# Two whole-array bf16 products of 512 columns ahead of every unit of scores and of second products in the narrow-head attention layers

## The chip, the cores and the metric

The kernel runs on one core of a Trainium2 chip. The metric is device microseconds of one execution; lower is better. The core has TensorE (PE in the profile, its weight loads PEld), VectorE (DVE), ScalarE (ACT), GpSimd (POOL) and SyncE (SP, which issues the DMAs).

## What is computed

Twelve decoder blocks in a row on x of shape (4, 256, 256), each followed by `x = layernorm(x + block(x))`. Two of the twelve are self-attention with sixteen narrow heads, and these two are what the change touches. In block 0 (L0_attn) a head has 16 features; with `scale = 1/sqrt(16)`:

```python
scores = einsum('bhqd,bhkd->bhqk', q, k) * scale
scores = where(causal, scores, -inf)
out = einsum('bhqk,bhkv->bhqv', softmax(scores), v) @ w_proj + b_proj
```

Block 6 (L2_attn) is differential attention: 16 heads with two sets of queries and keys of 8 features each, so 32 causal score matrices per sequence, `diff = A1 - lam * A2`, a root-mean-square over the 16 features of each head, and a projection. The other ten blocks (two state-space scans, four wide attentions, four feed-forwards) stay as they are.

## The kernel before

All five engines run through the blocks in the same order and meet in semaphores. Each engine's queue is in program order. The class `SmallHeads` serves block 0 (name L0a, 4 groups of four heads, width 16) and block 6 (name L2a, 8 groups of four, width 8). A unit is one group of four heads on one sequence of 256 tokens: 16 units in L0a, 32 in L2a. Each unit has four PSUM banks, and `slot = 4 * (u % 2)` swaps the lower four and the upper four between neighbouring units.

First comes a loop of `score(u)` over all units, which finds the largest score of each row. TensorE waits until VectorE has reduced unit u - 2 (`maxed`), writes the causal mask into the four banks with four bf16 products of the identity with `causal_bf`, 256 columns each (L386), and adds eight fp32 score products (L389; the trace has two instructions for each fp32 product). Those use only 16 (L0a) or 8 (L2a) of the 128 rows of the array; four of them stand side by side, one in each strip of 32 rows. VectorE takes the maxima in two reductions (L490). After every four units `turn_max` transposes the maxima (L395), ScalarE copies them (L551), and SyncE moves them by DMA into row `width` of the queries, so that the second scores come out less their maximum.

Then comes a loop in which `score_t(u + 1)` stands ahead of `sum_up(u)`. `score_t` (L414) writes transposed scores, again on 17 or 9 rows in four strips; it waits for `exped` and for `sum_read`, VectorE's copy (L498) of the sums of unit u - 2. ScalarE exponentiates (L558), GpSimd zeroes the masked half (L584), and `sum_up` (L425) multiplies by the values, with 128 rows and four strips of 32 columns. Its sums lie in columns 384 to 511 of the first two banks of the slot. After the loop the sums are transposed (L440), divided, transposed again, projected (L454) and handed to `LayerNorm`.

Ahead of both loops stand the query and key projections (L364) and the value projections (L369), which are whole-array fp32 products. Elsewhere in the kernel, in block 11, twelve bf16 products of 512 columns with the identity (L1916) stand between small products.

Of the kernel before, what the change touches and what calls it, by code (L numbers as in the profile page):

```python
# [26 lines left out]
P = 128  # L27
# [16 lines left out]
class Chain:  # L44


    def __init__(self, sem):
        self.sem, self.n, self.base = sem, 0, None
# [51 lines left out]
def bcast(ap, axis, n):  # L100

    shape = list(ap.shape)
    return ap.unsqueeze(axis).broadcast_to(shape[:axis] + [n] + shape[axis:])
# [139 lines left out]
class SmallHeads:  # L243
# [10 lines left out]
    def __init__(self, e, l, arena, name, groups, width, scale, diff):  # L254
        self.e, self.l, self.name = e, l, name
        self.groups, self.width, self.scale, self.diff = groups, width, scale, diff
        self.per_block, self.units = 32 // width, 4 * groups
        a, big = arena, e.big
        a.reset(), big.reset()
        self.qk_w = a.take(groups, 2, CH, P)  # L260
        self.v_w = a.take(CH, D)
        self.proj_w = a.take(CH, D)
        self.probs_t = a.take(2, 4, 4 * P)
        self.compact_w = self.probs_t.rearrange("p u j t -> p (u j t)")[:, 0:8 * P].rearrange("p (k s c f) -> p k s c f", k=2, s=2, c=CH)
        self.inv = a.take(2, 32)
        if not diff:
            self.qk_b = a.take(2, 2)
            self.v_b = a.take(D)
            self.proj_b = a.take(D)
        self.q = big.take(groups, TOKENS)  # L270
        self.k = big.take(groups, TOKENS)
        q_words = self.q.rearrange("p g t -> p (g t)")
        k_words = self.k.rearrange("p g t -> p (g t)")
        self.v = big.take(TILES, 16, 32)
        self.stage = big.take(2, 2, TOKENS)
        self.out_first = big.take(TOKENS)
        self.max_cols = big.take(2, 4, TILES)
        self.max_rows = big.take(groups, P, parts=32)
        self.att = k_words[:, 0:TILES * 64 * groups].rearrange("p (t d) -> p t d", t=TILES)
        self.att_t = q_words[:, (groups - 2) * TOKENS:groups * TOKENS].rearrange("p (c t) -> p c t", c=CH)  # L280
        self.att_out = self.att
        if diff:
            self.att_out = k_words[:, 4096:6144].rearrange("p (t d) -> p t d", t=TILES)
            self.sq = k_words[:, 6144:8192].rearrange("p (n d) -> p n d", d=16)
            self.lam_in = a.take(4, width)
            self.lam_prod = a.take(2, width)
            self.lam_dot = a.take(2)
            self.lam_exp = a.take(2)
            self.lam = a.take(1)
            self.ms = a.take(TILES * 16)  # L290
            self.rms = a.take(TILES * 16)
        self.n_loads = 16 * (4 if diff else 5 + 4 * groups)
        s = e.sem
        self.w_loaded, self.prepared = s(name + "_w_loaded"), s(name + "_prepared")
        self.cleared, self.x_biased = s(name + "_cleared"), s(name + "_x_biased")
        self.v_psum, self.v_ready = s(name + "_v_psum"), s(name + "_v_ready")
        self.proj_psum, self.staged = s(name + "_proj_psum"), s(name + "_staged")
        self.moved = [s(f"{name}_moved{b}") for b in range(2)]
        self.scored, self.maxed = s(name + "_scored"), s(name + "_maxed")
        self.max_psum, self.max_read, self.rows_moved = s(name + "_max_psum"), s(name + "_max_read"), s(name + "_rows_moved")  # L300
        self.scored_t, self.exped, self.masked = s(name + "_scored_t"), s(name + "_exped"), s(name + "_masked")
        self.summed, self.sum_read = s(name + "_summed"), s(name + "_sum_read")
        self.turned, self.normed = s(name + "_turned"), s(name + "_normed")
        self.att_t_psum, self.att_t_ready = s(name + "_att_t_psum"), s(name + "_att_t_ready")
        if diff:
            self.lam_dots, self.lam_exps = s(name + "_lam_dots"), s(name + "_lam_exps")
            self.diffed, self.squared = s(name + "_diffed"), s(name + "_squared")
            self.msq, self.rooted, self.att_ready = s(name + "_msq"), s(name + "_rooted"), s(name + "_att_ready")
# [44 lines left out]
    def tensor(self, pe):  # L353
        e, nc, l = self.e, self.e.nc, self.l
        B, G, mm = e.bank, self.groups, self.e.nc.tensor.matmul
# [17 lines left out]
        def score(u):  # L373
            g, b = divmod(u, 4)
            slot = 4 * (u % 2)
            if u < 2:
                pe.wait_ge(*((self.v_ready, 4) if u else (self.staged, 8)))
            else:
                pe.wait_ge(self.maxed, u - 1)
            if b == 0 and g % self.per_block == 0:  # L380
                pe.wait_ge(self.moved[g // self.per_block], 16 * 8 * self.per_block)
            if b == 1 and g:
                pe.wait_ge(self.max_read, g)
            for j in range(4):
                blocks = B[slot + j][:, 0:3 * P].rearrange("p (a b) -> p a b", b=P)
                mm(blocks[:, 0:3:2, :], e.ident_bf[:], bcast(e.causal_bf[:, P:2 * P], 1, 2), start=True, stop=False, skip_group_check=True)  # L386
            for h in range(2):
                for j in range(4):
                    last = mm(B[slot + j][:, h * P:(2 * h + 1) * P], self.q[self.rows(j), g, b * SEQ + h * P:b * SEQ + (h + 1) * P],  # L389
                              self.k[self.rows(j), g, b * SEQ:b * SEQ + (h + 1) * P], start=False, stop=True, skip_group_check=True)  # L390
            last.then_inc(self.scored, 1)
# [5 lines left out]
        for u in range(self.units):  # L397
            score(u)
            if u % 4 == 0 and u:
                turn_max(u // 4 - 1)  # L400
        turn_max(G - 1)

        def score_t(u):
            g, b = divmod(u, 4)
            slot = 4 * (u % 2)
            if u == 0:
                pe.wait_ge(self.rows_moved, 16 * 4 * (G + 1))
            if u >= 2:
                pe.wait_ge(self.exped, 2 * (u - 2) + 2)
                pe.wait_ge(self.sum_read, u - 1)  # L410
            for kc in range(2):
                for j in range(4):
                    rows = self.rows(j, 1)
                    last = mm(B[slot + j][:, kc * SEQ:kc * SEQ + (2 - kc) * P], self.k[rows, g, b * SEQ + kc * P:b * SEQ + (kc + 1) * P],  # L414
                              self.q[rows, g, b * SEQ + kc * P:(b + 1) * SEQ], start=True, stop=True, skip_group_check=True)
            last.then_inc(self.scored_t, 1)

        def sum_up(u):
# [8 lines left out]
            last.then_inc(self.summed, 1)  # L427

        score_t(0)
        for u in range(self.units):  # L430
            if u + 1 < self.units:
                score_t(u + 1)
            sum_up(u)
# [1783 lines left out]
```

## Time and profile before

| | |
|---|---|
| time, median of 3 runs | 2746.41 us (2738.42 to 2749.94) |
| profiled execution, own time | 2746.3 us |
| its span | 2744.5 us |
| mean granted TensorE clock | 0.803 |
| TensorE matmul busy | 2074.4 us (76%) |
| VectorE busy | 1602.8 us (58%) |
| ScalarE busy | 787.7 us (29%) |
| GpSimd busy | 570.8 us (21%) |

L0a lies at about 24 to 170 us of the span and L2a at about 885 to 1175 us. Rows of groups and timelines name a line, an engine, an operation and its output and inputs, then the count. [...] Busy time of TensorE counts an instruction from its start to its modelled end, whatever part of the array it fills. Times are microseconds unless marked ns.

### The profile page before, as it was taken

To read this page: it belongs to the slowest core of one execution; us is meant where nothing else is said; L and a number is where in the kernel's file an instruction comes from. 1 tells how busy PE (TensorE), PEld (TensorE's weight loads), DVE (VectorE), ACT (ScalarE), POOL (GpSimd) and SP (SyncE) were. 2 spreads that over 40 slices of the span, in tenths; PEclk is the share of its full clock that TensorE was granted. 3 is DMA by queue.
4 is the path that set the end of the run, shared out by engine and by line. 5 is a ranking of instruction groups with operands and counts; after the bars stand their busy time and mean duration, and the time that the engine had idled before them with its cause. 6 is when DMAs were issued, how large, how long until landed. Compare 5 with 4: busy or idle time off the path is not lost.

```text
span 2744.5 us, 27737 instructions
## 1 busy us (share of the span) xinstructions
PE 2074.4 (76%) x9734; PEld 1308.8 (48%) x9734; DVE 1602.8 (58%) x2454; ACT 787.7 (29%) x1999; POOL 570.8 (21%) x325
## 2 busy tenths in 40 slices
PE   6774659746636888788888974454799999999986
PEld 3541234412213446566666743333566675555843
DVE  3259965879977441445555339999366514444214
ACT  1233311233312014355555211111255403444010
POOL 1212530005410003233333115655100000000010
PEclk9566879658867655689999986776799999999966
DMA  3000011010010210000001010000000100000000
GB/s 99 6 32 0 0 15 37 5 48 0 0 39 3 32 41 1 1 20 11 11 11 54 1 69 0 0 0 0 4 10 10 43 8 12 11 11 20 1 31 16
DMA packets 25727, 48.98 MB, mean 18 GB/s; under 512 B 6262, under 2 KB 19603, under 8 KB 24092
## 3 DMA queue, kind: packets, MB, share of 16 engines
q1 hardware_dynamic: 25644, 47.85, 5.8%
q8 instruction: 55, 0.90, 0.1%
q14 instruction: 28, 0.23, 0.0%
HBM read 42.20 MB, written 1.05 MB: 16 GB/s over the span
## 4 chain that ended last, share of the span: by engine, by line
PE 55%; DVE 34%; ACT 4%; issue 4%; SPq 1%; POOL 1%; DMA 1%; DVEq 0%; ACTq 0%; POOLq 0%
DVE big L789 7%; PE banks L1110 7%; PE banks L1079 7%; PE banks L1119 6%; PE banks L1048 6%; DVE big L1790 5%; PE banks L1102 3%; PE banks L414 3%; DVE big L1786 3%; PE banks L389 3%; PE banks L425 2%; PE banks L1344 2%; PE banks L386 2%; DVE big L784 2%; DVE big L770 1%
## 5 line engine op out<-in xcount | busy, mean ns | idle before, releaser
L1185 DVE COPY arena<-banks 128x512 f32<-128x512 f32 x196 | 135.5, 691 | 329.4 <-PE banks L1102 326.3
L218 POOL TENSOR_TENSOR ln_rstd<-ln_var_eps,neg_half 128x2 f32<-128x2 f32 x48 | 36.9, 768 | 1065.5 <-DVE ln_var_eps L206 1065.5
L1079 PE MATMUL banks<-big 128*128 128x256 f32 x784 | 235.7, 413 | 6.0 <-ACT big L1221 4.4
L1110 PE MATMUL banks<-arena,big 128*128 128x256 f32 x784 | 227.7, 414 | 6.3 <-DVE arena L1185 6.3
L1242 ACT ACTIVATE arena<-banks,arena 128x256 f32<-128x256 f32 x392 | 193.4, 500 | 61.0 <-DVE arena L1159 43.1
L789 DVE TENSOR_TENSOR_SCAN big<-big 128x2048 f32<-128x2048 f32 x32 | 203.4, 6355 | 1.1
L701 PE MATMUL banks<-big,ident 128*128 128x512 f32 x288 | 171.3, 750 | 38.1 <-POOL big L862 38.1
L862 POOL TENSOR_TENSOR big<-big 128x2048 f32<-128x2048 f32 x32 | 144.8, 4525 | 251.7 <-DVE big L789 251.7
L1048 PE MATMUL banks<-x_feat,arena 128*128 128x512 f32 x392 | 176.3, 592 | 0.0
L1119 PE MATMUL banks<-arena,big 128*128 128x256 f32 x784 | 174.3, 382 | 1.9 <-ACT big L1260 1.9
L1260 ACT ACTIVATE big<-banks 128x256 f32 (+1 forms) x196 | 75.3, 384 | 347.9 <-PE banks L1110 347.9
L1110 PEld LDWEIGHTS banks<-arena,big 128*128 128x128 f32 x784 | 140.8, 197 | 64.5 <-DVE arena L1185 42.9
L1166 DVE TENSOR_SCALAR arena<-arena 128x256 f32<-128x256 f32 x392 | 166.0, 466 | 6.9
L1153 DVE TENSOR_REDUCE arena<-banks 128x2 f32<-128x512 f32 x196 | 134.0, 684 | 61.6 <-PE banks L1079 43.5
L1119 PEld LDWEIGHTS banks<-arena,big 128*128 128x128 f32 x784 | 147.5, 190 | 27.5 <-issue 4.6
L1750 PE MATMUL banks<-ident,big 128*128 128x128 f32 x128 | 30.0, 426 | 161.8 <-POOL big L1839 161.8
L1079 PEld LDWEIGHTS banks<-big 128*128 128x128 f32 x784 | 136.1, 201 | 33.9 <-ACT big L1221 8.8
L1790 DVE SCALAR_TENSOR_TENSOR big<-big,arena 128x2048 f32<-128x2048 f32 x32 | 141.2, 4411 | 1.1
L1102 PE MATMUL banks<-ident,arena 128*128 128x128 f32 x784 | 127.4, 288 | 17.1 <-DVE arena L1166 17.1
L199 DVE TENSOR_TENSOR x_tok<-x_tok,banks 128x512 f32<-128x512 f32 x48 | 32.8, 683 | 182.6 <-PE banks L1119 100.1
L701 PEld LDWEIGHTS banks<-big,ident 128*128 128x128 f32 x288 | 66.9, 243 | 134.7 <-issue 75.7
L234 ACT ACTIVATE x_feat<-banks 128x512 f32<-128x512 f32 x48 | 27.8, 594 | 355.6 <-PE banks L226 355.6
(311 smaller groups left out, 3706.7 us busy)
## 6 DMA issues: line engine op xcount, KB each, us to landing
big<-big SPq DMA_DIRECT2D x32, 64.0 KB, 2.3
arena<-in_L0f_w SPq DMA_DIRECT2D x1, 2048.0 KB, 8.1
arena<-in_L1a_wo SPq DMA_DIRECT2D x1, 2048.0 KB
arena<-in_L1f_gv SPq DMA_DIRECT2D x1, 2048.0 KB
arena<-in_L2a_qk_w SPq DMA_DIRECT2D x1, 2048.0 KB
big<-big SPq DMA_DIRECT2D x64, 32.0 KB
arena<-in_L2x_wo SPq DMA_DIRECT2D x1, 2048.0 KB
arena<-in_L2x_q_w SPq DMA_DIRECT2D x16, 128.0 KB, 2.0
```

Source lines behind the costliest of these rows:

```text
L701: last = nc.tensor.matmul(B[4 + q][:], e.ident[:], self.out[k][:, q * BANK:(q + 1) * BANK], start=False, stop=False, skip_group_check=True)
L789: v.tensor_tensor_scan(self.state[k], self.decay[k], self.drive, 0.0, ALU.mult, ALU.add).then_inc(self.s_scanned, 1)
L862: self.e.nc.gpsimd.tensor_tensor(halves(self.out[k]), halves(self.state[k]), bcast(self.c_all[k], 1, CH), ALU.mult).then_inc(self.s_outed, 1)
L1048: last = mm(B[half][:], self.q_w[:, head_par, c, :], e.x_feat[:, c, cols], start=(c == 0), stop=(c == CH - 1))
L1079: last = mm(ps[:, h * SEQ:(h + 1) * SEQ], q[:, b * SEQ + h * P:b * SEQ + (h + 1) * P], k[:, b * SEQ:(b + 1) * SEQ], start=True, stop=not s ...
L1102: last = nc.tensor.transpose(B[4 + u % 2][:, kc * SEQ + h * P:kc * SEQ + (h + 1) * P], self.probs[:, u % 2, h, kc * P:(kc + 1) * P], e.ide ...
L1110: last = mm(slot, self.v[:, 2 * b + kc, :], self.probs_t[:, u % 2, kc, :], start=(kc == 0), stop=(kc == 1))
L1119: last = mm(e.y_bank(t), self.out[:, h, t * P:(t + 1) * P], wo[h], start=(h == 0), stop=(h == self.heads - 1 and not self.bias))
L1166: last = v.tensor_scalar(self.probs[:, u % 2, h, :], self.probs[:, u % 2, h, :], self.inv[:, u % 2, h:h + 1], None, ALU.mult)
L1185: v.tensor_copy(self.probs_t[:, u % 2].rearrange("p a b -> p (a b)"), B[4 + u % 2][:]).then_inc(self.turn_read, 1)
L1242: last = a(self.probs[:, u % 2, h, :], B[2 + u % 2][:, h * SEQ:(h + 1) * SEQ], ACT.Exp, bias=self.neg_max[:, u % 2, h:h + 1], scale=scale, ...
L1790: v.scalar_tensor_tensor(self.chosen[h], self.sums, self.final[:, h, 7:8], self.sums, ALU.is_ge, ALU.mult, accum_out=self.kept[:, h:h + 1] ...
```

## The change

Ahead of the mask products of each `score(u)`, and ahead of the products of each `score_t(u)`, behind that unit's waits in both cases, TensorE now makes two bf16 products of the identity with the causal block repeated four times, 128 rows by 128 columns by 512 columns each. They go to the first two banks of the slot, with `start=True`; the products behind them overwrite what is read later. Nothing waits for them by semaphore, and no wait is added or removed. In L0a that is 2 x 32 products, in L2a 2 x 64.

```diff
         self.inv = a.take(2, 32)
+        self.warm = bcast(e.causal_bf[:, P:2 * P], 1, 4)
         if not diff:
...
             if b == 1 and g:
                 pe.wait_ge(self.max_read, g)
+            for j in range(2):
+                mm(B[slot + j][:], e.ident_bf[:], self.warm, start=True, stop=True)
             for j in range(4):
                 blocks = B[slot + j][:, 0:3 * P].rearrange("p (a b) -> p a b", b=P)
...
             if u >= 2:
                 pe.wait_ge(self.exped, 2 * (u - 2) + 2)
                 pe.wait_ge(self.sum_read, u - 1)
+            for j in range(2):
+                mm(B[slot + j][:], e.ident_bf[:], self.warm, start=True, stop=True)
             for kc in range(2):
                 for j in range(4):
                     rows = self.rows(j, 1)
```

## Rows read from the trace of the kernel before

**Rows 1.** The page: span, and TensorE busy and its granted clock in 40 slices.
```profile
span 2744.5 us, 27737 instructions
...
PE   6774659746636888788888974454799999999986
...
PEclk9566879658867655689999986776799999999966
```

**Rows 2.** Windows of the narrow layers: stretch, length, busy by engine, clock, DMA share.
```profile
47.90:57.40 9.50, 7.76 (x104) 4.46 (x103) 8.68 (x12) 0.27 (x1) 0.00 (x0) 1.00 0.33 57
57.40:87.00 29.60, 28.61 (x222) 15.06 (x220) 19.07 (x22) 0.53 (x2) 0.00 (x0) 0.50 0.01 3
98.00:152.00 54.00, 44.35 (x580) 32.55 (x572) 6.37 (x15) 21.23 (x29) 18.40 (x30) 0.50 0.01 2
915.40:1003.00 87.60, 84.36 (x647) 44.66 (x647) 56.52 (x62) 1.87 (x7) 0.00 (x0) 0.50 0.09 14
1014.00:1126.00 112.00, 92.86 (x1204) 68.69 (x1200) 12.74 (x30) 44.16 (x59) 37.90 (x60) 0.50 0.03 11
```

**Rows 3.** Timeline of L2a's score loop: start, length, engine, line, idle before and releaser.
```profile
915.51 1.01 PE L386 MATMUL banks<-causal_bf,ident_bf 128*128 128x256 bf16 x4 [6.73 <-DMA big<-big]
...
918.05 1.03 PE L386 MATMUL banks<-causal_bf,ident_bf 128*128 128x256 bf16 x4
919.01 1.67 PE L389 MATMUL banks<-big 8*128 8x128 f32 x16
920.61 1.03 PE L386 MATMUL banks<-causal_bf,ident_bf 128*128 128x256 bf16 x4
920.74 1.82 DVE L490 TENSOR_REDUCE big<-banks 128x4 f32<-128x512 f32 x2 [0.74 <-PE banks L389]
```

**Rows 4.** Timeline of L0a's score loop at the full clock, with one `turn_max`, and its end.
```profile
47.94 0.60 PE L386 MATMUL banks<-causal_bf,ident_bf 128*128 128x256 bf16 x4
49.34 0.61 PE L386 MATMUL banks<-causal_bf,ident_bf 128*128 128x256 bf16 x4
51.35 0.61 PE L386 MATMUL banks<-causal_bf,ident_bf 128*128 128x256 bf16 x4 [0.54 <-DVE big L490]
53.08 0.61 PE L386 MATMUL banks<-causal_bf,ident_bf 128*128 128x256 bf16 x4 [0.25 <-DVE big L490]
53.62 0.94 PE L389 MATMUL banks<-big 16*128 16x128 f32 x16
54.81 0.61 PE L386 MATMUL banks<-causal_bf,ident_bf 128*128 128x256 bf16 x4 [0.25 <-DVE big L490]
57.27 0.80 PE L386 MATMUL banks<-causal_bf,ident_bf 128*128 128x256 bf16 x4 [0.45 <-ACT big L551]
...
85.24 1.67 PE L389 MATMUL banks<-big 16*128 16x128 f32 x16
```

**Rows 5.** Timeline of the second loop: its start in L0a, one round in L2a.
```profile
93.42 2.94 PE L414 MATMUL banks<-big 17*128 17x256 f32 x32 [4.18 <-DMA big<-big]
97.42 0.87 PE L425 MATMUL banks<-arena,big 128*32 128x128 f32 x12 [1.05 <-POOL arena L584]
...
1053.24 1.66 PE L414 MATMUL banks<-big 9*128 9x256 f32 x16 [0.64 <-DVE big L498]
1054.84 1.51 PE L425 MATMUL banks<-arena,big 128*32 128x128 f32 x24
1054.96 1.51 ACT L558 ACTIVATE arena<-banks 128x768 f32<-128x768 f32 x2 [2.23 <-PE banks L414]
1056.41 0.42 DVE L498 COPY big<-banks 128x256 f32<-128x256 f32 x1 [3.32 <-PE banks L425]
```

**Rows 6.** Timeline of block 11: whole-array products (L1908, L1916) beside products of one row (L1909).
```profile
2628.53 2.08 PE L1908 MATMUL banks<-arena,x_feat 128*128 128x256 f32 x4
2630.54 1.22 PE L1909 MATMUL banks<-arena,ones 1*128 1x256 f32 x2
2631.69 2.08 PE L1908 MATMUL banks<-arena,x_feat 128*128 128x256 f32 x4
...
2647.48 4.81 PE L1916 MATMUL banks<-arena,ident_bf 128*128 128x512 bf16 x12
```

**Rows 7.** Windows: block 11's alternation, and L2a's projections in two stretches.
```profile
2621.00:2646.00 25.00, 24.74 (x51) 13.00 (x50) 2.82 (x3) 3.37 (x5) 2.59 (x2) 0.50 0.00 0
885.40:890.40 5.00, 4.97 (x6) 2.18 (x7) 0.00 (x0) 2.08 (x3) 3.51 (x1) 0.50 0.13 30
890.40:908.00 17.60, 17.60 (x57) 10.48 (x56) 2.27 (x6) 4.18 (x7) 0.00 (x0) 1.00 0.27 41
```

## The prediction

> **What bounds the kernel now.** I read the page first. TensorE is the busiest engine, and its granted clock is far from full in several slices [rows 1]. Two of the low stretches are the narrow-head layers, so I read windows over them [rows 2]. L0a's score loop begins at clock 1.00 and runs at 0.50 from 57.4 us on; its second loop, and both loops of L2a, run at 0.50 throughout. In the score loops TensorE is busy nearly all the time (84.36 of 87.60 us in L2a) while VectorE has gaps: TensorE is the bound there. In the second loops TensorE is busy 92.86 of 112.00 us, so the timeline has to say what fills the rest.
>
> In a score unit at 0.50 the mask products start at 918.05, the narrow products at 919.01 and the next unit's mask at 920.61: 0.96 + 1.60 = 2.56 us, with no wait of TensorE, and VectorE idle 0.74 us before its 1.82 us [rows 3]. At clock 1.00 a unit takes 1.73 us (53.08 to 54.81), and TensorE waits 0.25 us of it for VectorE [rows 4]. The second loop is one closed chain through two engines: L414 starts at 1053.24, L425 at 1054.84, VectorE copies at 1056.41 for 0.42 us, and the next L414 would start 0.15 us later, at 1056.98. A round is 1.60 + 1.57 + 0.57 = 3.74 us [rows 5]. ScalarE's 1.51 us runs beside L425 and has 2.23 us of idle before it, so it sets nothing.
>
> **The change part by part.** Each unit gets 1024 more whole-array bf16 columns in each loop. At 0.50 their price is in the mask products, which are 1024 columns of the same operand and take 0.96 us up to the start of the narrow ones [rows 3]. That holds one switch from whole array to strips, which the added pair shares with the mask behind it. Twelve products of 512 columns, at 0.50 up to a rise near their end, take 4.81 us with their tail, 0.80 a pair at least [rows 6]. In the score loop the switch is shared, so the price lies below 0.96, and the last of the twelve ran at the higher clock, so it lies above 0.80: I take 0.85, nearer to the row with the same shape, bounds 0.80 and 0.96. In the second loop nothing whole-array stands behind the pair, so the switch comes on top where the wait for VectorE hid it before: 0.94, bounds 0.85 and 1.05. At full clock I take half, 0.43. None of it can be hidden by a wait in steady state: TensorE's queue is in order, and the pair stands behind the unit's waits and ahead of products that others wait for. A gain below nothing is possible only through the clock, which is the whole question.
>
> *Does the clock rise?* What counts isn't how busy TensorE is: it is busy over 95% of L2a's score loop at 0.50 [rows 2]. The nearest row is in block 11: four whole-array products for 2.01 us, then two on one row for 1.15 us, round after round, 24.74 of 25.00 us busy, and the clock stays at 0.50 [rows 6, 7]. There 64% of the time goes to whole-array work. With the change, a score unit of L2a has 0.85 + 0.96 = 1.81 us of whole-array work in 3.41 us, 53%, and the rest on 8 rows of each strip. That is less than the row that stays low. On the other side, uninterrupted whole-array work is at 0.50 for 5.00 us and at 1.00 after it [rows 7], and the twelve L1916 products in block 11 are uninterrupted too. L2a's first unit comes after 6.73 us of waiting for a DMA [rows 3], so it starts low and I expect it to stay low to the end of its scores. In its second loop a round becomes 4.68 us: the pair is 0.85 us of that, L425's column strips 1.57 with their tail, L414 on 9 rows 1.60, and the round trip to VectorE still 0.57 idle. I expect 0.50 there as well, and in L0a's second loop, which starts after 4.18 us of DMA wait [rows 5].
>
> L0a's score loop differs. It comes straight from whole-array projections at 1.00 and held it for five units with the mask alone [rows 2, 4]. There the pair doubles the whole-array columns of a unit while the unit hardly grows, so I expect the full clock to hold to its end. The unit's length there follows from the loop over two buffers: two units took 3.46 us (51.35 to 54.81); with 0.43 more ahead of the mask, 3.89, so 1.94 a unit. TensorE's own work would be 1.40 (47.94 to 49.34) + 0.43 = 1.83, less than that. A `turn_max` adds 2.46 - 1.73 = 0.73 [rows 4]. The loop ends at 47.94 + 15 x 1.94 + 3 x 0.73 + 0.43 + 1.48 (53.08 to the end of L389) = 81.1, against 85.24 + 1.67 = 86.9 now: 5.8 us less. What follows is the same transpose, copy and DMA.
>
> [...]
>
> *The sum.* L0a scores -5.8. L0a second loop 15 x 0.94 = +14.1; one of its 16 pairs, unit 1's, is hidden in the 1.05 us in which TensorE waits for GpSimd before the first L425 [rows 5]. L2a scores 32 x 0.85 = +27.2. L2a second loop 31 x 0.94 = +29.1. Together +64.6 us. The profiled execution took 2746.3 us (span 2744.5 and 1.8 around it), the median of the runs is 2746.41, so both give 2811. DMA waits ahead of and between the loops keep their length, since what they wait for moves with them.
>
> **The rivals.** A, the other sign: the pairs lift the clock in all four loops. It decides as soon as the clock is granted once in a loop, since at full clock the same pairs fill a larger share of a shorter unit, and it would hold from there. Scores in L2a go from 2.56 to 1.94 a unit, 32 x -0.62 = -19.8, with 7 turns at 0.1 more each; a round of the second loop from 3.74 to about 2.9 (1.60 and 1.57 lose the half of their streaming, about 0.64 each, and 0.43 comes in), 46 x -0.84 = -38.6. With L0a's -5.8: -63.5, 2683. For it: the clock did hold in L0a while whole-array work was in every unit. Against it: the loops start low, and a row with a larger whole-array share stays low.
>
> B: only L0a's second loop is lifted; it has 17 rows where L2a has 9, and is the nearest to it. Then 15 x -0.84 = -12.6 in place of +14.1: +37.9, 2784.
>
> C: L0a's score loop doesn't hold the full clock either; it falls as now. Then it costs 16 x 0.85 = +13.6 (less at its start) in place of -5.8: +84, 2830. Against it: the pair is the same kind of work that held it for five units.
>
> D: the pairs cost next to nothing, hidden in the 0.57 us round trip and VectorE's slack: 2746, no change. Against it: the order of the queue, as above. The price bounds (0.80 to 0.96 for 32 pairs, 0.85 to 1.05 for 46) move the forecast by -6 to +9 us.
>
> **How the numbers follow.** Forecast 2811 with chance 0.76; A 0.06; B 0.08; C 0.06; D and the rest 0.04. The forecast's own range is 2800 to 2822: the bounds of the prices, and the phase at which the clock changes in the later layers, for which the 11.5 us between the runs of before are the measure. Reaching to B leaves out less than 0.2: 2782 to 2823. A change of 0.5% is 14 us, about what a measurement of this kernel can tell from none. Slower by more: forecast, B, C and some of the rest, 0.91. Faster: A, 0.07. Same: 0.02.
>
> **What the profile after would show.** Right: L2a's score unit at 3.41 us with no wait of TensorE and clock 0.50 over the whole loop; the second loop's round at 4.68 us with the VectorE copy's releaser unchanged; L0a's scores at 1.00 up to about 81 us, units of 1.94. Wrong: clock 1.00 inside L2a's loops (A), or in L0a's second loop alone (B); a fall of the clock before 81 us (C); L414 starting sooner than 0.85 us behind the first added product (D). What would undo the forecast is one thing: that narrow or strip-wise products count for more towards the clock than the block 11 row lets me think.

## The result

| | before | after |
|---|---|---|
| time, median | 2743.44 us (4 runs, 2738.42 to 2749.94) | 2814.75 us (4 runs, 2810.12 to 2816.47) |
| profiled execution: time, span | 2746.3, 2744.5 us | 2810.12, 2808.3 us |
| mean granted clock, as a share of full speed | 0.803 | 0.800 |
| TensorE matmul busy | 2074.4 us | 2140.7 us |
| VectorE busy | 1602.8 us | 1602.5 us |

The ratio is 1.0256, with a 95% interval of 1.0228 to 1.0284: 2.6% slower. The forecast was 2811 us. The medians are 71.3 us apart and the profiled executions 63.8 us.

The page of the kernel after, the same rows as [rows 1]; lines in between are left out:

```profile
span 2808.3 us, 28121 instructions
...
PE   6874669746636888878888885544599999999986
...
PEclk9566879668867555578888998777699999999966
```

Windows of the kernel after over the stretches of [rows 2] (stretch, length, busy of TensorE, its weight loads, VectorE, ScalarE and GpSimd, clock, DMA share and GB/s): L0a's scores, its second loop, L2a's scores, its second loop.

```profile
47.30:79.80 32.50, 30.42 (x356) 16.86 (x353) 27.98 (x32) 0.80 (x3) 0.00 (x0) 1.00 0.10 19
98.00:152.00 54.00, 46.58 (x476) 26.95 (x480) 4.92 (x12) 16.62 (x22) 14.55 (x23) 0.50 0.01 1
923.80:1039.00 115.20, 111.88 (x711) 54.38 (x711) 56.64 (x63) 1.86 (x7) 0.00 (x0) 0.50 0.07 11
1050.00:1190.00 140.00, 120.86 (x1264) 69.94 (x1260) 12.72 (x30) 45.36 (x60) 38.26 (x61) 0.50 0.02 8
```

One loop of the four has the full clock, L0a's scores, to their end; the other three are at 0.50 over the whole stretch, as before. The timeline of L2a's scores after, the counterpart of [rows 3]. The added pair is L386 here, the mask L389 and the narrow products L392:

```profile
927.20 1.03 PE L386 MATMUL banks<-causal_bf,ident_bf 128*128 128x512 bf16 x2
928.02 1.06 PE L389 MATMUL banks<-causal_bf,ident_bf 128*128 128x256 bf16 x4
929.01 1.67 PE L392 MATMUL banks<-big 8*128 8x128 f32 x16
930.61 1.03 PE L386 MATMUL banks<-causal_bf,ident_bf 128*128 128x512 bf16 x2
930.75 1.82 DVE L495 TENSOR_REDUCE big<-banks 128x4 f32<-128x512 f32 x2 [1.59 <-PE banks L392]
```

From pair to pair it is 3.41 us (2.56 before), TensorE doesn't wait in these units (only at each of the seven transposes of the maxima, 0.4 us, as before), and VectorE's idle before a unit has grown from 0.74 to 1.59 us, by the 0.85 that the pair takes. The second loop after, beside [rows 5]. The pair is L415, the scores L419, the sums L430:

```profile
121.80 1.01 PE L415 MATMUL banks<-causal_bf,ident_bf 128*128 128x512 bf16 x2 [0.64 <-DVE big L503]
122.74 1.66 PE L419 MATMUL banks<-big 17*128 17x256 f32 x16
124.33 1.51 PE L430 MATMUL banks<-arena,big 128*32 128x128 f32 x24
125.91 0.42 DVE L503 COPY big<-banks 128x256 f32<-128x256 f32 x1 [4.26 <-PE banks L430]
126.45 0.14 PEld L415 LDWEIGHTS banks<-causal_bf,ident_bf 128*128 128x128 bf16 x2 [1.06 <-ACT arena L563]
126.48 1.01 PE L415 MATMUL banks<-causal_bf,ident_bf 128*128 128x512 bf16 x2 [0.64 <-DVE big L503]
```

A round is 4.68 us where it was 3.74. The pair stands between the wait for VectorE's copy and the scores, and takes 0.93 to 0.94 us up to them.

Stage by stage, each from its first TensorE product to the first one of the next stage:

| stage | before | after | difference | forecast |
|---|---|---|---|---|
| L0a scores | 47.94 to 93.42: 45.5 | 47.15 to 86.45: 39.3 | -6.2 | -5.8 |
| L0a second loop | 93.42 to 154.23: 60.8 | 86.45 to 161.55: 75.1 | +14.3 | +14.1 |
| L2a scores | 915.51 to 1009.70: 94.2 | 923.80 to 1045.31: 121.5 | +27.3 | +27.2 |
| L2a second loop | 1009.70 to 1130.35: 120.7 | 1045.31 to 1195.29: 150.0 | +29.3 | +29.1 |
| sum | | | +64.7 | +64.6 |

The profiled executions differ by 63.8 us, so all that is left for the rest of the kernel is -0.9. The medians differ by 7.5 us more than that. The profiled execution after is the fastest of its four and the profiled one before is above its median, and the times before spread over 11.5 us; which stages the other executions differ in was not traced.

### The profile page after: what moved, and what is told of

It is laid out like the page before. It is cut to its first block, busy times and chain, and to the rows that moved or that the text cites. A ratio compares the mean times of both kernels' runs of the same rounds, so it can differ in the third digit from the quotient of the medians.

```text
span 2808.3 us, 28121 instructions
## 1 busy us (share of the span) xinstructions
PE 2140.7 (76%) x9926; PEld 1319.4 (47%) x9926; DVE 1602.5 (57%) x2454; ACT 787.5 (28%) x1999; POOL 570.4 (20%) x325
## 4 chain that ended last, share of the span: by engine, by line
PE 56%; DVE 33%; issue 3%; ACT 3%; SPq 1%; POOL 1%; DMA 1%; DVEq 0%; ACTq 0%; POOLq 0%
DVE big L794 7%; PE banks L1115 7%; PE banks L1084 7%; PE banks L1124 6%; PE banks L1053 6%; DVE big L1795 5%; PE banks L1107 3%; PE banks L419 3%; DVE big L1791 3%; PE banks L430 2%; PE banks L392 2%; PE banks L1349 2%; PE banks L415 2%; DVE big L789 1%; DVE big L775 1%
## 5 line engine op out<-in xcount | busy, mean ns | idle before, releaser
L1265 ACT ACTIVATE big<-banks 128x256 f32 (+1 forms) x196 | 75.1, 383 | 347.9 <-PE banks L1115 347.9
L503 DVE COPY big<-banks 128x256 f32<-128x256 f32 x48 | 20.4, 424 | 213.7 <-PE banks L430 213.7
L589 POOL TENSOR_SCALAR_AFFINE_SELECT arena<-arena 128x512 f32<-128x512 f32 x96 | 60.9, 634 | 371.8 <-ACT arena L563 368.6
```

## The experiments

The forecast held, but its reason was my argument from neighbouring rows, which no row shows by itself: that whole-array work is what the clock goes by, that a pair a unit is too little to lift it, and that it might hold it. The rivals say that narrow loops stay low whatever stands between (so each product is only a price), or that only pauses, in which TensorE waits, take the clock away. All edits below are against the changed kernel unless said otherwise, and products are of the pair's kind.

**The pairs in L0a's scores alone.** The second loops' pairs are gone, and L2a's scores have none.

```diff
-            for j in range(2):
-                mm(B[slot + j][:], e.ident_bf[:], self.warm, start=True, stop=True)
+            for j in range(0 if self.diff else 2):
+                mm(B[slot + j % 2][:], e.ident_bf[:], self.warm, start=True, stop=True)
...
-            for j in range(2):
-                mm(B[slot + j][:], e.ident_bf[:], self.warm, start=True, stop=True)
```

> The pairs stand in the score loop of L0a alone; all other loops are as before. My theory: this is the one loop in which they pay, because it comes straight from the projections at the full clock and the pairs keep it there. L0a's scores end 5 to 6 us sooner (last score product at about 80 us instead of 86.9), the rest of the layer runs as before, and the time is about 6 us under the kernel before, 2737. Rival (the pairs only cost their own time, and the earlier end in the changed kernel came from something else): 16 x 0.43 to 0.85 us more, 2750 to 2757.

The window over L0a's scores:

```profile
47.50:80.00 32.50, 30.42 (x355) 16.86 (x353) 28.03 (x32) 0.80 (x3) 0.00 (x0) 1.00 0.10 19
```

The stage did as expected: full clock to the end, the last score product at 80.2 us. The time did not: 2749.33 us (10 runs, 2748.45 to 2750.57) against 2750.81 for before (19 runs on the same chip, 2736.58 to 2756.65), ratio 0.9991, 0.9974 to 1.0008. No gain is measured, where I had expected 2737. In its profile the first sums of L0a are turned at 147.4 us instead of 154.2, and L2a still begins 2.1 us later, at 887.5 instead of 885.4: the gain went between the two layers. The next run shows where most of it went.

**The kernel before once more**, nothing changed. It was run to see whether block 3, a stage between the two layers that the change doesn't touch, varies by itself.

> The kernel before, profiled once more, with nothing changed. My theory: the blocks between L0a and L2a hold stretches whose clock depends on where in time they fall, so that the same instructions take several us more or less; the third attention (L1a, block 3), 69.0 us in the profile of before and of the changed kernel and 74.6 us in four experiments, should take one of these two times here as well, with the narrow layers at 45.5 and 60.8 us (L0a) as before. Rival (the edits of the experiments made block 3 slower): 69.0 here.

2750.04 us. Windows of this profile: L0a's scores in two parts, and the end of block 3 (L1a), output products that alternate with bias products of one row. Under them, block 3's end in the first profile of before.

```profile
46.50:64.60 18.10, 14.88 (x202) 8.45 (x201) 16.42 (x20) 0.53 (x2) 0.00 (x0) 1.00 0.18 32
64.60:80.80 16.20, 15.75 (x124) 8.29 (x121) 10.94 (x12) 0.27 (x1) 0.00 (x0) 0.50 0.01 4
541.00:557.20 16.20, 15.40 (x36) 7.80 (x36) 9.39 (x28) 1.79 (x3) 3.06 (x4) 0.50 0.00 1
```

```profile
545.00:555.80 10.80, 9.95 (x33) 5.56 (x32) 9.35 (x28) 1.82 (x4) 2.87 (x4) 0.69 0.01 2
```

The loop of scores and the second loop of L0a in this profile begin with these:

```profile
46.22 0.60 PE L386 MATMUL banks<-causal_bf,ident_bf 128*128 128x256 bf16 x4
...
87.31 1.24 PE L414 MATMUL banks<-big 17*128 17x256 f32 x8 [4.17 <-DMA big<-big]
```

Two things come out. Block 3 took 74.5 us in this run, from its input's last copy into `x_feat` to its output's, and 69.1 in the first profile, with the same instructions: its end ran at 0.50 here (541.0 to 557.2 us) and partly at 1.00 there (1.00 from 541.0 to 548.0, 0.50 from 550.0 to 555.8). So the experiments' edits did not slow it, and that half of my theory holds. The other half doesn't: I expected L0a as in the first profile, and its scores held the full clock for 18.4 us from their start instead of 9.5, and took 41.1 us (46.22 to 87.31) instead of 45.5. They also began 1.7 us sooner, so their end, at 80.8 instead of 86.9, is no measure of the loop. The gain of about 6 us that I forecast for the pairs in L0a's scores is against one execution in which the clock fell early; against this one it is 41.1 - 39.3 = 1.8 us. What all six profiles with pairs there show is the clock held to the end of that loop, in 39.3 us. What that is worth in time depends on when the clock would have fallen.

**Six products ahead of each unit, in all four loops.** Three times the added work. The same edit stands in both loops:

```diff
-            for j in range(2):
-                mm(B[slot + j][:], e.ident_bf[:], self.warm, start=True, stop=True)
+            for j in range(6):
+                mm(B[slot + j % 2][:], e.ident_bf[:], self.warm, start=True, stop=True)
...
```

> Six products of 512 columns ahead of each unit in all four loops, three times what the change has. My theory: the clock goes by how much of a stretch is whole-array work, so six lift it from 0.50 inside every loop, and all four run at 1.00 after a few units. Then TensorE's part of a score unit is 1.40 + 6 x 0.213 = 2.68 us (2.56 at 0.50 without any), a round of the second loop is about 2.45 + 1.28 = 3.73 us (3.74 at 0.50 without any); with some units at 0.50 at each loop's start the time is 2750 to 2775: three times the added work, and 40 to 60 us faster than the pairs. Rival (narrow loops stay at 0.50 whatever stands between, every product is paid at 0.43 us): 64 units of 6 x 0.427 = 2.56 us in L2a and 16 in L0a's second loop, 1.3 in L0a's scores: 2743 + 220 = 2965.

2781.05 us, one run, beside 2750.81 for before. It is 6 us above my range, and 184 below the rival's 2965. Windows: both loops of L0a, then of L2a, each from where the clock is high:

```profile
50.00:93.00 43.00, 41.66 (x399) 21.91 (x401) 27.36 (x30) 0.80 (x3) 0.00 (x0) 1.00 0.06 11
112.60:166.00 53.40, 43.56 (x665) 25.80 (x663) 5.94 (x14) 21.17 (x28) 17.84 (x28) 1.00 0.01 2
945.40:1032.00 86.60, 83.46 (x803) 44.07 (x799) 54.72 (x60) 1.87 (x7) 0.00 (x0) 1.00 0.06 10
1051.20:1163.00 111.80, 92.52 (x1377) 54.51 (x1375) 12.72 (x30) 45.34 (x60) 37.58 (x59) 1.00 0.01 2
```

The expectation's 0.213 and 0.427 us a product stand on no row as such. The runs show 0.216 at 1.00 (thirty in a row in the next run's bridge take 6.64 us, the last of them 0.38) and 0.42 at 0.50 (this run's first six in L2a's scores take 2.72, the last of them 0.61).

This is the clearest run against "each product is only a price". With six, the clock rises by itself 9.0 to 12.4 us into each of the three loops that start low, and stays. Nor does the busy share decide it here. TensorE is busy 96% of L2a's score loop here at 1.00 (83.46 of 86.60 us), as it was before at 0.50 (84.36 of 87.60), and in the stretch ahead of the rise it is no busier than in the changed kernel, whose clock stays low (this run first):

```profile
936.40:945.40 9.00, 8.95 (x40) 3.96 (x44) 1.82 (x2) 0.00 (x0) 0.00 (x0) 0.50 0.30 47
```

```profile
924.00:937.00 13.00, 13.00 (x88) 6.58 (x86) 5.47 (x6) 0.00 (x0) 0.00 (x0) 0.50 0.33 51
```

Two rounds of L2a's second loop:

```profile
1102.84 1.46 PE L415 MATMUL banks<-causal_bf,ident_bf 128*128 128x512 bf16 x6 [0.64 <-DVE big L503]
1104.23 0.94 PE L419 MATMUL banks<-big 9*128 9x256 f32 x16
1105.09 0.86 PE L430 MATMUL banks<-arena,big 128*32 128x128 f32 x24
1106.59 1.46 PE L415 MATMUL banks<-causal_bf,ident_bf 128*128 128x512 bf16 x6 [0.64 <-DVE big L503]
```

A round is 3.75 us with 3072 added columns at the full clock, 4.68 with 1024 at the half, and 3.74 with none. The pair is the dose between: in the three loops that start low it pays its price and gets nothing back. The starts of the loops don't explain the time above my range: the four stages together are 26.4 us longer than in the profile of before, and the spans 34.6. The other 8.2 us lie in the rest of the kernel, 5.6 of them in block 3, which is at the longer of its two times here.

Every product added in these experiments is of one kind, whole-array, bf16 and 512 columns long. No run adds products on few rows, or fp32 ones, so that the rows count, and not the type or the length, is argued from block 11 and not shown.

**Bridges over the pauses, with the pairs and without.** The changed kernel with products in the time in which TensorE waits ahead of the low loops:

```diff
+            for j in range((30 if self.diff else 0) if u == 0 else 0):
+                mm(B[j % 4][:], e.ident_bf[:], self.warm, start=True, stop=True)
             if b == 0 and g % self.per_block == 0:
                 pe.wait_ge(self.moved[g // self.per_block], 16 * 8 * self.per_block)
...
+        pe.wait_ge(self.maxed, self.units - 1)
+        for j in range(8):
+            mm(B[j % 4][:], e.ident_bf[:], self.warm, start=True, stop=True)
         turn_max(G - 1)
...
+            for j in range((18) if u == 0 else 0):
+                mm(B[j % 4][:], e.ident_bf[:], self.warm, start=True, stop=True)
             if u == 0:
                 pe.wait_ge(self.rows_moved, 16 * 4 * (G + 1))
```

> The changed kernel with more products of the same kind in the three pauses ahead of the low loops: 30 ahead of the DMA wait before L2a's first unit of scores, and in both layers 8 ahead of the last transpose of the maxima and 18 ahead of the DMA wait before the second loop. They fill time in which TensorE waits now. My theory: a pair a unit can't lift the clock but can hold it, so with the pause bridged all four loops run at 1.00: scores 1.94 us a unit, rounds of the second loop about 2.9, and the time is 2744 - 63 = 2681 (2675 to 2700, since a bridge may run a little long). Rival (work on 8 to 17 rows of a strip pulls the clock down also with pairs): the clock falls within a few units of each loop, and the time is that of the changed kernel, 2805 to 2820.

2742.76 us (10 runs, 2738.38 to 2769.54) against 2750.81, ratio 1.0001, 0.9966 to 1.0036: no difference measured, where the changed kernel was 71 us above its own before. Seven of the ten runs lie between 2738 and 2743; the other three, 2758 to 2770, have a lower mean clock (0.818 to 0.823 against 0.830 to 0.832) and bring the ratio to 1. They were not traced. Windows: L0a's two loops, L2a's scores, L2a's second loop from 982.3 us.

```profile
48.00:80.60 32.60, 30.51 (x355) 16.86 (x353) 28.12 (x32) 0.80 (x3) 0.00 (x0) 1.00 0.10 19
87.70:134.00 46.30, 34.89 (x655) 22.57 (x658) 6.36 (x15) 24.08 (x32) 20.30 (x32) 1.00 0.02 5
905.90:971.00 65.10, 60.38 (x702) 33.36 (x705) 56.12 (x62) 1.86 (x7) 0.00 (x0) 1.00 0.11 18
982.30:1125.00 142.70, 122.66 (x1292) 71.08 (x1288) 13.16 (x31) 45.45 (x61) 38.82 (x62) 0.50 0.03 9
```

Three of the four loops hold 1.00 once they start there, two of them with the same pairs that couldn't lift it. L2a's second loop holds it for less than 5 us, then runs rounds of 4.68 us as in the changed kernel. I had expected all four, 2681; the loop that fell takes 27.6 us more than before, in place of a gain of about 26. The bridge behind L0a's scores cost nothing at the high clock: from the last score product to the second loop it is 6.4 us, as in the changed kernel, and TensorE still waits 0.29 us for the DMA.

The same bridges and no pairs in any loop:

> The bridges of the run before, and no pairs in any loop. My theory: scores need the pairs to hold the clock, so L0a's and L2a's score loops fall to 0.50 after a few units, as L0a's did before (at 57.4 us, after five units). The second loops have 128-row products in column strips; L0a's, with 17 rows beside them, may hold, L2a's, with 9 rows, should fall. Time 2720 to 2745. Rival (only the pauses take the clock away, the pairs do nothing): all loops hold 1.00 once bridged, 1.73 us a score unit and 2.45 a round: 2744 - 27 - 59 = 2658, faster than the run with pairs.

2754.69 us, one run, 10 us above my range. L0a's scores to the fall, then L2a's scores, to the fall and behind it:

```profile
46.80:52.00 5.20, 4.41 (x62) 2.55 (x61) 4.38 (x7) 0.00 (x0) 0.00 (x0) 1.00 0.51 89
927.00:932.70 5.70, 4.91 (x69) 2.87 (x70) 4.38 (x6) 0.00 (x0) 0.00 (x0) 1.00 0.33 52
932.70:1011.00 78.30, 75.16 (x583) 39.76 (x579) 51.98 (x57) 1.86 (x7) 0.00 (x0) 0.50 0.07 12
```

With the pause bridged and nothing more, L2a's scores have 5.7 us at the full clock and fall among the narrow units. L0a's second loop fell too, at 99.8 us after 3.7 us, where I had thought it might hold, and L2a's second loop at 1021.4 us, 2.3 us after its start. L0a's scores, whose instructions are those of before, fell at 52.0 us, the earliest of the three profiles without pairs: they took 40.9 us from the first mask to the end of the last score, against 39.0 and 34.6 in the two profiles of before and 32.9 with pairs. The bridge behind them began at 0.50, and the second loop started 8.3 us after the last score, where it was 6.5 before. The four stages together are as long as in the profile of before, 321 us. The rival that only pauses count (2658) falls.

The pause itself shows at the start of the loop: L2a's scores start at 0.50 behind the wait of 6.67 us in the changed kernel and at 1.00 behind the bridge. This run shows that the bridge isn't enough, with the fall 5.7 us later. The six-product run shows that it isn't needed either where the loop has enough added work: its L2a scores begin at 0.50 behind a wait of 6.76 us and rise by themselves.

**The bridges with one product a unit in all loops.**

> The bridges, and one product a unit in place of two in all loops. My theory: L0a's loops hold 1.00 still (16 and 17 rows), with scores of 1.84 us; L2a's scores (8 rows) hold between the transposes of the maxima but fall at one of the first of them, and L2a's second loop falls at its start as with pairs, 4.25 us a round at 0.50. L2a's scores fallen are 2.99 us a unit. Time 2755 to 2765. Rival (any whole-array product at all holds the clock once it is high, and only the start of L2a's second loop was at fault): L2a's scores stay at 1.00 over the whole loop.

2769.75 us, one run, 5 us above my range. L0a's second loop and L2a's scores, to the fall and behind it:

```profile
85.40:91.10 5.70, 3.91 (x72) 2.83 (x74) 0.42 (x1) 2.92 (x4) 2.55 (x4) 1.00 0.16 38
91.10:150.00 58.90, 49.70 (x585) 31.96 (x581) 5.95 (x14) 21.16 (x28) 17.84 (x28) 0.50 0.00 1
922.00:941.00 19.00, 16.92 (x212) 9.41 (x211) 16.04 (x18) 0.53 (x2) 0.00 (x0) 1.00 0.32 50
941.00:1010.00 69.00, 66.76 (x465) 33.95 (x467) 40.12 (x44) 1.33 (x5) 0.00 (x0) 0.50 0.02 4
```

L2a's scores held for 19 us and two transposes of the maxima and fell then, as expected; L0a's scores held to their end. L0a's second loop did not hold, against my expectation; L2a's second loop fell at its start, as expected. One product holds less than two: two held L2a's scores to their end in all four profiles that have them behind a bridge (73.0 us each), and L0a's second loop in both that have two from its first unit on (48.0 us each). In these loops the amount counts, not that there is any.

**More held: the bridges, and more in the second loops.** Six products ahead of the first two units of each second loop, where TensorE waits for GpSimd, and three a round in L2a's:

```diff
-            for j in range(2):
-                mm(B[slot + j][:], e.ident_bf[:], self.warm, start=True, stop=True)
+            for j in range(6 if u < 2 else 3 if self.diff else 2):
+                mm(B[slot + j % 2][:], e.ident_bf[:], self.warm, start=True, stop=True)
             for kc in range(2):
```

> The bridged kernel with pairs, with three products a unit in L2a's second loop in place of two and six ahead of the first two units of each second loop, where TensorE waits for GpSimd. My theory: L2a's second loop fell to 0.50 at 982.3 us because its first rounds hold a wait and its 9-row products bring little, so a little more whole-array work holds it: rounds of 3.1 us, 32 x (3.74 - 3.1) = 20 us under the kernel before, with the 20 us of L0a and 21 us of L2a's scores that the bridged run showed: 2750 - 60 = 2690 (2680 to 2705). Rival (the 9-row loop can't be held): it falls again, with three products a round at 0.50 of 5.1 us, 2760 to 2775.

2694.21 us (6 runs) against 2747.87 for before on the same chip (11 runs), ratio 0.9815, 0.9779 to 0.9851. Of the six runs one took 2718.77 us, the others 2692.17 to 2696.0. L2a's second loop:

```profile
980.00:1078.00 98.00, 78.12 (x1353) 48.74 (x1352) 13.18 (x31) 48.23 (x64) 39.99 (x63) 1.00 0.07 25
```

It is at 1.00 to its end, in rounds of 3.10 us (two of the triples start at 1040.75 and 1043.85 us), with more filler than the changed kernel has in that loop. Against their own before, this version is 53.7 us lower and the changed kernel 71.3 us higher. It is faster than the kernel before, by 1.5 to 2.2%, so whether by a full 2% is open; with the changed kernel it was not run side by side, but the distance is far beyond any spread seen.

Which of the two additions did it? First the start alone, with pairs in the later rounds; then three a round from the first unit, with no extra start.

> The run with more held, less its third product a round in L2a's second loop: six products ahead of the first two units of each second loop, pairs ahead of all others. It tells which of the two additions held that loop. My theory: both matter; with pairs alone a round of 2.89 us has whole-array or 128-row work in most of it, so the loop outlives its start, but it may fall later, since its rounds bring the least of all. If it holds to the end: L2a's second loop about 31 x 2.9 + 5 = 95 us, and the time 2685 to 2692. If it falls at once: about 148 us and 2740 (the start isn't the cause). Between: it falls on the way.

> The run with more held, less its six products ahead of the first two units: three a round in L2a's second loop from its first unit on, two in L0a's. My theory: two more columns blocks in the first two units are most of what the start needs, since the loop fell there with pairs by little; it holds, L2a's second loop takes about 99 us, the time is 2690 to 2697. Rival (the wait for GpSimd in the first round takes the clock away whatever the rounds have later): it falls in the first 5 us, rounds of 5.1 us, L2a's second loop 163 us, and the time is 2755.

2735.36 and 2744.28 us, one run each, beside 2740.48 for before. L2a's second loop in the first, then in the second of them:

```profile
978.50:991.90 13.40, 10.82 (x189) 6.88 (x188) 1.70 (x4) 7.36 (x10) 5.54 (x9) 1.00 0.43 171
991.90:1120.00 128.10, 110.56 (x1158) 64.27 (x1158) 11.47 (x27) 41.03 (x55) 35.28 (x56) 0.50 0.01 1
```

```profile
966.50:970.10 3.60, 2.88 (x48) 1.99 (x51) 0.00 (x0) 2.52 (x4) 1.41 (x3) 0.99 0.84 350
970.10:1126.00 155.90, 135.84 (x1326) 76.12 (x1321) 13.20 (x31) 45.85 (x61) 39.36 (x62) 0.50 0.02 8
```

Both fall. The first does so on the way, 14.8 us after the loop's start at 977.1 us. The second falls 4.4 us after its start, in the first sums behind the wait for GpSimd, as the rival to my expectation had it:

```profile
968.09 0.94 PE L426 MATMUL banks<-big 9*128 9x256 f32 x16
969.74 1.26 PE L437 MATMUL banks<-arena,big 128*32 128x128 f32 x24 [0.72 <-POOL arena L596]
971.62 1.44 PE L422 MATMUL banks<-causal_bf,ident_bf 128*128 128x512 bf16 x3 [0.62 <-DVE big L510]
```

In these runs it took both, one to get over the wait in the first round, the other to live through the later rounds. Each is a single execution, and where a loop falls moved between executions of the same kernel (57.4 and 64.6 us in L0a's scores before), so how much margin each addition leaves is open.

The stages of all profiles, in us, with block 3, which no edit touches:

| profile | L0a scores | L0a second | L2a scores | L2a second | block 3 |
|---|---|---|---|---|---|
| before | 45.5 | 60.8 | 94.2 | 120.7 | 69.1 |
| before once more | 41.1 | 60.8 | 94.2 | 120.7 | 74.5 |
| pairs in L0a's scores alone | 39.3 | 60.8 | 94.2 | 120.7 | 74.6 |
| changed kernel | 39.3 | 75.1 | 121.5 | 150.0 | 69.1 |
| six products | 52.0 | 66.2 | 102.4 | 126.9 | 74.6 |
| bridges and pairs | 39.3 | 48.0 | 73.0 | 148.2 | 74.6 |
| bridges alone | 49.3 | 59.7 | 92.3 | 119.9 | 74.6 |
| bridges, one product | 37.5 | 66.2 | 97.5 | 135.5 | 74.6 |
| bridges, more held | 39.3 | 49.6 | 73.0 | 102.3 | 74.6 |
| of that, the start only | 39.3 | 48.9 | 73.0 | 143.5 | 74.5 |
| of that, three a round only | 39.3 | 48.0 | 73.0 | 161.6 | 69.1 |

## Why the prediction was right

*The bound.* TensorE bounds the score loops, and the closed chain of TensorE and VectorE the second ones; every 0.85 and 0.94 us added at 0.50 came out in full (3.41 and 4.68 us, both as forecast). The pair of unit 1 was hidden but for some 0.2 us: 14.3 and 29.3 us are 15.2 and 31.2 times 0.94, not 16 and 32.

*The price.* 0.85 between the bounds 0.80 and 0.96, and 0.94 with the switch to strips, came out within a hundredth of a microsecond. The switch shows in the profile after: from a pair to the mask, which is whole-array too, it is 0.82 us (927.20 to 928.02; the mask then takes 0.99 where it took 0.96), and from a pair to the narrow scores 0.94 (121.80 to 122.74). So was the unit at full clock: the pairs in L0a start at 50.99, 52.84 and 54.85 us, 1.85 and 2.01, mean 1.93 for the 1.94 of the two-buffer loop. The 0.64 us that rival A takes off each half of a round stand on no row; from 0.50 to 1.00 the scores of L2a's second loop went from 1.66 to 0.94 and its sums from 1.51 to 0.86. The prices of the rivals came out near all the same: where a bridge gave the clock, L0a's second loop came out 12.8 us shorter than before (12.6 in B) and L2a's scores 21.2 (about 19 in A).

*The clock.* The step on which everything hung, that the three loops which start low stay low, is right in the profile after. Its reason has two halves. That busy time alone doesn't decide is shown by L2a's scores, which rise with six products (8.95 of 9.00 us busy ahead of the rise) and stay low with two (13.00 of 13.00). That whole-array work is what counts is my estimate: no run contradicts it, but the kind of the added products was never varied, so it was not shown. The forecast needed less, that a pair is too little, and the profile after shows that; the runs with bridges add what I had left as the condition of rival A: L2a's scores with the same pairs ran at 0.50 to their end where they started at 0.50, and at 1.00 to their end where they started at 1.00. I gave A a chance of 0.06 as if a single grant anywhere would carry it; L2a's second loop, which started at 1.00 behind its bridge, fell with pairs within 5 us, and with six products at its start after 14.8.

*The term that was luck in part.* L0a's -5.8 was measured as -6.2 and is right against the profiled execution. The second profile of before has L0a's scores 4.4 us shorter by itself, and against it the term is -1.8. How large it is against the median execution isn't known, and the run with this term alone measured no gain at all; the sum of 65 hides that. The total owes something to the same spread: the forecast adds 64.6 us to 2746.4 and meets a median of 2814.75, but the medians are 71.3 us apart. Of rivals B, C and D the changed kernel shows nothing: no clock of 1.00 in L0a's second loop, no fall in its scores, no pair for nothing.

## What to carry to other kernels

Price filler products at both clocks (here a pair was 0.85 to 0.94 us at 0.50, and in L0a's scores made a unit 1.93 us in place of 1.73 at 1.00), and ask of each loop which clock it starts at before asking whether filler helps: a dose too small to raise the clock is paid in full at the low one (+64 us here), and the same dose held it in two of the three loops whose pause was bridged. A bridge in the time in which TensorE waits for a DMA cost nothing here while the clock was high (6.4 us from L0a's scores to its second loop, with it and without); begun at the low clock it ran 1.8 us over (8.3 for 6.5). Add until the loop holds and check every loop's window for the granted clock, its first round with its waits above all; the total time doesn't show which loop failed. And compare stages, not totals, when a few microseconds matter: here a stage gained 6 us and block 3 gave back 5.6 by the clock alone, and of the last two runs the one whose second loop was 18 us longer took only 9 us more.

## What the runs showed that I had not expected

The low clock doesn't come with the narrow products alone: the same L2a score loop, with the same pairs, ran at 0.50 for 115 us in the changed kernel and at 1.00 for 65 us behind a bridge. A kernel with unchanged instructions has stretches that come out at either clock: block 3 took 69.1 or 74.5 us, L0a's scores fell at 57.4 or 64.6 us, and 19 runs of the kernel before spread from 2736.58 to 2756.65 us. The kernel with pairs in L0a's scores alone spread over 2.1 us in 10 runs at about the same median; why it is so much steadier was not tried.
